# All edges gathered by indirect DMAs in tiles of 120 rows, and the gather on TensorE taken out

## The chip, the cores and the metric

The program runs on one core of a Trainium2 chip. The metric is the device time of one execution in microseconds (us). The kernel before has a median of 1892.74 us in 3 runs (1892.62 to 1893.34).

## What is computed

One layer of attention over the edges of a graph with 6250 nodes and 206250 edges (sorted by destination), 64 features in 4 heads of 16, then a residual and a layer norm:

```python
Qh = (x @ Wq.T + bq).reshape(n, H, D)
Kh = (x @ Wk.T + bk).reshape(n, H, D)
Vh = (x @ Wv.T + bv).reshape(n, H, D)
Ee = (edge_attr @ We.T + be).reshape(-1, H, D)
score = (Kh[src] * Qh[dst] * (1.0 / np.sqrt(D)) * Ee).sum(-1)
score = jnp.exp(jnp.clip(score, -5.0, 5.0))
msg = Vh[src] * score[..., None]
wV = jax.ops.segment_sum(msg, dst, num_segments=n)
# result: _layernorm(x + wV)
```

`src` is random, so K and V of the source nodes must be gathered row by row; `dst` is sorted, so the destinations of a run of edges lie in a narrow window.

## The kernel before

**Three stages.** The first block projects all nodes, writes K and V as one table of 512-byte rows to HBM (`kv_table`) and Q as a second table (`q_table`), and starts the first gathers. The middle block goes over the edges. The last block normalizes and stores.

**Tiles and groups.** A tile is 128 edges, one to a partition. T = 8 tiles make a group; the 1612 tiles make 202 groups, the last of 4 tiles. Group g uses slot g % 4 of four buffers (`kv`, `attr_sb`, `q_win`, `onehot`, `idx`).

**Two ways to gather.** GpSimd issues one indirect DMA for each tile: 128 rows of `kv_table` chosen by one column of `idx` (line 275, in `gather`). In slots 0, 1 and 3 the eighth tile of a group is not gathered by GpSimd: TensorE makes it by a product with a one-hot matrix over all 49 x 128 nodes (`pe_tile`, line 255). For such a tile VectorE makes the one-hot in four parts (line 803), TensorE multiplies it with the node features kept in three bf16 parts (49 products, line 675), turns the result (line 683) and projects it (line 689), and ScalarE copies between these steps (lines 765, 770, 776) and into `kv`. So GpSimd issues 1464 gathers, 7.25 for a group on average.

**What sets the order.** Each engine has its own hand-written order, and semaphores join them. GpSimd walks through the groups in order (line 612): for group g + 4 it waits for `slot_ready`, which VectorE raises when it has made the messages of group g and copied the new indices into `idx` (line 303). VectorE in group g waits for the slot's gathers (`kv_gathered`), for the tile of TensorE (`pe_kv_made`) and for the Q rows (`qe_made`), then does kq (824), adds the sums of the group before to `acc` (813), kqe (830), the reduction (835), the clip (839), waits for the exponential on ScalarE (772), makes the messages (844) and copies the indices. TensorE in group g makes the edge features and the turned one-hot of group g + 1 (625 to 633), fetches its Q rows (646) and sums the messages of group g (656). SyncE loads edge attributes and Q windows ahead, four slots deep.

**Around the middle block.** In the first block GpSimd issues 17 gathers of the first three groups (EARLY) and one reduction over partitions between them; it is the last engine to finish that block. `x_parts`, `columns`, `src_f` and `minus_first` serve the gather on TensorE alone and are made there on ScalarE, VectorE and GpSimd (lines 341, 418, 447 to 453, 524, 528).

Of the kernel before, what the change touches and what calls it, by code (L numbers as in the profile page):

```python
# [23 lines left out]
T = 8  # L49
PAIRS = T // 2  # L50
TILES = -(-E // P)
# [16 lines left out]
PE_TILES = ITERS * (SLOTS - 1) - 2  # L68
PARTS = tuple(slice(-(-NT * p // 4), -(-NT * (p + 1) // 4)) for p in range(4))
HALVES = (slice(0, (NT + 1) // 2), slice((NT + 1) // 2, NT))  # L70

PARTS_AT = (((0, 0), (0, 1), (0, 2)), ((0, 3), (1, 0), (1, 1)), ((1, 2), (1, 3), (2, 0)), ((2, 1), (2, 2), (2, 3)))
DONE_AT = (-1, None, 0, 1)
# [3 lines left out]
def gnn_kernel(nc, xT, x_own_rows, w_kvq, We_t, be_row, src_tab, dst_tab, dst_first, attr, out):  # L77
    ctx = ExitStack()
    with ctx:
# [6 lines left out]
        def sem(name):  # L86
# [9 lines left out]
        x_parts = sb("x_parts", [P, NT, 3, F], BF16)  # L96
# [10 lines left out]
        src_f = sb("src_f", [P, GPAD * T], F32)  # L107
        minus_first = sb("minus_first", [P, P], F32)
        columns = sb("columns", [P, NT, P], BF16)
# [6 lines left out]
        xg_t_sb = sb("xg_t_sb", [P, P], F32)  # L116
# [6 lines left out]
        x_own, x_rest = (kv_stage[:].rearrange("p t f -> p (t f)")[:, s * NT * F:(s + 1) * NT * F]  # L123
                         .rearrange("p (t f) -> p t f", f=F) for s in range(2))
# [15 lines left out]
        column_i = sb("column_i", [P, NT], I32, first)  # L140
        minus_first_i = sb("minus_first_i", [P, P], I32, first)
# [5 lines left out]
        xg_banks = [ps(f"xg_bank{i}", [P, 4, P], F32) for i in range(2)]  # L147
# [5 lines left out]
        src_ps = ps("src_ps", [P, 8, P], BF16)[:, 0, :]  # L153
        p_ps = sum_ps[:, 2, 0:T * H]
        xg_ps = [b[:].rearrange("p a b -> p (a b)")[:, 0:3 * F].rearrange("p (s f) -> p s f", s=3) for b in xg_banks]
        xg_t_ps = [b[0:F, 2, :] for b in xg_banks]
        xg_kv_ps = [b[:, 3, :] for b in xg_banks]

        kv_banks = [ee_ps[0], ee_ps[1], qe_ps, xg_banks[0]]
        q_banks = [oht_bank, sum_ps, xg_banks[1]]  # L160
# [16 lines left out]
        x_own_loaded = sem("x_own_loaded")  # L177
        x_part0 = sem("x_part0")
        x_rested = sem("x_rested")
        x_part1 = sem("x_part1")  # L180
        x_part2 = sem("x_part2")
# [5 lines left out]
        ident_zeroed = sem("ident_zeroed")  # L187
        ident_set = sem("ident_set")
        iota_set = sem("iota_set")
        column_set = sem("column_set")  # L190
# [48 lines left out]
        src_seen_made = sem("src_seen_made")  # L239
        src_turned = sem("src_turned")  # L240
        src_onehot_made = sem("src_onehot_made")
        x_gathered = sem("x_gathered")
        x_kept = sem("x_kept")
        x_turned = sem("x_turned")
        x_turned_kept = sem("x_turned_kept")
        kv_projected = sem("kv_projected")
        pe_kv_made = sem("pe_kv_made")
        window_moved = sem("window_moved")
        pass_sems = range(attr_loaded[0].num, window_moved.num + 1)
        assert len(pass_sems) == 3 * SLOTS + 26  # L250
# [4 lines left out]
        def pe_tile(g, slot):  # L255

            return slot != 2 and not (isinstance(g, int) and (g < 3 or g >= ITERS * SLOTS))

        def gathered_before(slot, turn):

            if isinstance(turn, int) and turn == 0:
                return 0
            if slot == 2:
                return turn * T

            return turn * (T - 1) + (1 if slot < 2 else 0)

        def pool_tiles(g, slot):

            return T - 1 if pe_tile(g, slot) else 2 * pairs_of(g)  # L270

        def gather(pool, g, slot, first=0, end=T):

# [6 lines left out]
        def is_tile(q):  # L280

            return not isinstance(q, int) or 0 <= q < PE_TILES

# [748 lines left out]
```

## Time and profile before

| | |
|---|---|
| median of 3 runs | 1892.74 us |
| span of the profiled execution | 2801.3 us |
| busy in it: PE, DVE, ACT, POOL | 1925.7, 1174.3, 851.7, 1400.8 us |
| gathers by GpSimd | 1464 |
| mean granted TensorE clock | 0.771 |

The profiled execution took 908.6 us longer than the median of the plain runs, far more than the runs differ among themselves. So a reader has to keep two things apart: the length of one instruction in it, and the waits between instructions, which need not be those of a plain run. PE stands for TensorE's products and PEld for its weight loads, DVE for VectorE, ACT for ScalarE, POOL for GpSimd, SP for SyncE. A gather counts as busy on POOL while GpSimd works on issuing it, 946 ns on average; its data moves later.

### The profile page before, as it was taken

The page shows a single profiled execution, that of the slowest core. Times are in us where ns is not written, and L with a number is a line of the kernel's source. Part 1 is how long each engine was busy: PE and PEld are TensorE (multiplying, and loading weights), DVE is VectorE, ACT ScalarE, POOL GpSimd, SP SyncE. Part 2 cuts the span into 40 slices and gives each one's busy share as a digit, 9 for nine tenths or more (in the row PEclk, how much of TensorE's full clock was granted, in tenths as well). Part 3 has the DMA queues.
Part 4 walks back from the last instruction along what each step waited for, and adds up shares of the span by engine and source line. Part 5 has one row for each costly group of instructions (what it writes and reads, how often), then busy time and mean ns, then how long its engine had stood idle before and what let it go on. Part 6 is the DMA issues. An engine that isn't in the chain of part 4 may idle for free. (4 is left out here: it accounts for less than half of the span.)

```text
span 2801.3 us, 49920 instructions
## 1 busy us (share of the span) xinstructions
PE 1925.7 (69%) x16647; PEld 1663.0 (59%) x16647; DVE 1174.3 (42%) x2092; ACT 851.7 (30%) x2863; POOL 1400.8 (50%) x1495
## 2 busy tenths in 40 slices
PE   4666677777767667776767676667676667766775
PEld 4555666666656556665656665656565656655665
DVE  4433444444434444444444444434344444434444
ACT  6222222332223223223322222223232223222233
POOL 5444554455554445555445555445545545555443
PEclk7777777777778777787877877778778777778776
DMA  6222222222222222222222222222222222222221
GB/s 194 63 56 57 59 58 58 57 61 57 58 54 59 56 58 60 58 59 59 59 57 58 59 57 58 57 56 60 57 58 58 59 57 60 59 58 59 56 61 45
DMA packets 113024, 171.42 MB, mean 61 GB/s; under 512 B 59952, under 2 KB 60592, under 8 KB 112880
## 3 DMA queue, kind: packets, MB, share of 16 engines
q0 software_dynamic: 46848, 96.04, 13.5%
q1 hardware_dynamic: 66160, 75.18, 9.8%
q8 instruction: 9, 0.15, 0.0%
q14 instruction: 7, 0.06, 0.0%
HBM read 163.85 MB, written 7.23 MB: 61 GB/s over the span
## 5 line engine op out<-in xcount | busy, mean ns | idle before, releaser
L275 POOL DMA_INDIRECT kv<-kv_table,idx x1464 | 1384.4, 946 | 1351.1 <-DVE idx L303 944.9
L675 PE MATMUL xg_bank<-x_parts,src_onehot 128*128 128x192 bf16 x7252 | 904.6, 286 | 102.7 <-issue 99.1
L675 PEld LDWEIGHTS xg_bank<-x_parts,src_onehot 128*128 128x128 bf16 x7252 | 739.8, 115 | 187.4 <-issue 129.2
L803 DVE TENSOR_TENSOR src_onehot<-src_ps,columns 128x1664 bf16<-128x1664 bf16 (+1 forms) x592 | 573.0, 968 | 537.0 <-remote 359.3
L646 PE MATMUL qe_ps<-q_win,onehot_t 128*128 128x128 bf16 x2418 | 250.2, 267 | 407.2 <-issue 389.9
L646 PEld LDWEIGHTS qe_ps<-q_win,onehot_t 128*128 128x128 bf16 x2418 | 194.3, 120 | 441.2 <-issue 439.5
L735 ACT COPY onehot_t<-oht_bank 128x512 bf16<-128x512 bf16 x202 | 118.0, 584 | 1099.3 <-remote 1052.4
L743 ACT ACTIVATE distance<-iota_w,dst_neg 128x64 f32<-128x64 f32 x1612 | 405.9, 337 | 15.4 <-PEq L306 15.4
L656 PE MATMUL sum_ps<-onehot,msg 128*64 128x64 f32 x3224 | 357.7, 290 | 49.3 <-issue 42.4
L656 PEld LDWEIGHTS sum_ps<-onehot,msg 128*64 128x64 f32 x3224 | 319.8, 200 | 111.1 <-issue 93.8
L844 DVE TENSOR_TENSOR msg<-kv,sum_ps 128x512 f32<-128x512 f32 x202 | 138.0, 683 | 563.2 <-ACT sum_ps L772 497.0
L633 PEld LDWEIGHTS ee_ps<-we_sb,attr_sb 128*128 128x128 f32 x1612 | 225.3, 201 | 16.9 <-issue 10.6
L633 PE MATMUL ee_ps<-we_sb,attr_sb 128*128 128x128 f32 x1612 | 228.5, 284 | 8.8 <-issue 8.1
L689 PE MATMUL xg_bank<-w_sb,xg_t_sb 128*128 128x128 f32 x296 | 106.7, 460 | 142.8 <-ACT xg_t_sb L770 113.8
L813 DVE TENSOR_TENSOR acc<-acc,sum_ps 64x64 f32 x202 | 43.2, 214 | 373.7 <-PE sum_ps L656 286.4
L824 DVE TENSOR_TENSOR kq<-kv,qe_ps 128x512 f32<-128x512 f32 x202 | 137.3, 680 | 125.3 <-ACT kv L776 82.6
L689 PEld LDWEIGHTS xg_bank<-w_sb,xg_t_sb 128*128 128x128 f32 x296 | 69.1, 289 | 180.4 <-ACT xg_t_sb L770 148.1
L770 ACT COPY xg_t_sb<-xg_bank 64x128 f32<-64x128 f32 x148 | 38.2, 258 | 330.7 <-remote 311.3
L830 DVE TENSOR_TENSOR kqe<-kq,ee_ps 128x512 f32<-128x512 f32 x202 | 136.3, 675 | 1.1 <-issue 0.3
L835 DVE TENSOR_REDUCE score<-kqe 128x32 f32<-128x512 f32 x202 | 135.5, 671 | 0.1
L748 ACT ACTIVATE onehot<-distance 128x512 f32<-128x512 f32 x202 | 127.0, 629 | 6.4
L765 ACT CAST xg_sb<-xg_bank 128x192 bf16<-128x192 f32 x148 | 45.0, 304 | 242.6 <-remote 228.8
(117 smaller groups left out, 760.9 us busy)
## 6 DMA issues: line engine op xcount, KB each, us to landing
attr_sb<-attr SPq DMA_DIRECT2D x201, 256.0 KB
kv<-kv_table,idx POOLq DMA_INDIRECT x1464
q_win<-q_table SPq DMA_DIRECT2D x404, 24.0 KB
kv_table<-kv_stage SPq DMA_DIRECT2D x7, 448.0 KB, 3.6
q_table<-q_stage SPq DMA_DIRECT2D x7, 336.0 KB
xT_sb<-xT SPq DMA_DIRECT2D x7, 224.0 KB, 4.8
kv_stage<-x_own_rows SPq DMA_DIRECT2D x1, 1568.0 KB
out<-y_sb SPq DMA_DIRECT2D x5, 256.0 KB, 2.0
```

Of the source, the lines that this page charges most:

```text
L275: pool.indirect_dma_start(out=kv[:, slot, t, :], out_offset=None, in_=kv_table, in_offset=bass.IndirectOffsetOnAxis(ap=idx[:, slot, t:t + ...
L633: mm = pe.matmul(ee[:, k * P:(k + 1) * P], attr_sb[:, slot, k * P:(k + 1) * P], we_sb[:, :], start=False, stop=(k == n - 1))
L646: mm = pe.matmul(bank(qe_ps, n * P)[:, k * P:(k + 1) * P], onehot_t[:, k, :], q_win[:, slot, :, s, :], start=(s == 0), stop=(s == 2))
L656: mm = pe.matmul(sum_ps[0:F, slot % 2, 0:W], msg[:, slot % 2, t, :], onehot[:, slot, t, :], start=(t == 0), stop=(t == n - 1))
L675: mm = pe.matmul(xg_ps[k % 2], src_onehot[:, c, :], x_parts[:, c, :, :], start=(c == 0), stop=(c == NT - 1))
L689: pe.matmul(xg_kv_ps[k % 2], xg_t_sb[:, :], w_sb[:, 0:2 * F], start=True, stop=True)\
L743: last = act.activation(distance[:, t, :], iota_w[:, :], ACT.Square, bias=dst_neg[:, ds(g, 1), t:t + 1].rearrange("p o t -> p (o t)"))
L803: dve.tensor_tensor(src_onehot[:, PARTS[part], :], src_ps.unsqueeze(1).to_broadcast([P, n, P]), columns[:, PARTS[part], :], ALU.is_equal). ...
L824: dve.tensor_tensor(kq[:, 0:n, :], kv[:, slot, 0:n, 0:F], qe_ps[:, 0:n, :], ALU.mult).then_inc(kq_made, 1)
L830: dve.tensor_tensor(kqe[:, 0:n, :], kq[:, 0:n, :], ee_ps[slot % 2][:, 0:n, :], ALU.mult).then_inc(kqe_made, 1)
L835: dve.tensor_reduce(score[:, 0:n * H], kqe[:, 0:n, :].rearrange("p t (h d) -> p (t h) d", d=D), AX_X, ALU.add).then_inc(score_summed, 1)
L844: dve.tensor_tensor(msg[:, slot % 2, 0:n, :].rearrange("p t (h d) -> p t h d", d=D), kv[:, slot, 0:n, F:2 * F].rearrange("p t (h d) -> p t ...
```

## The change

A tile has R = 120 edges, in partitions 0 to 119 of the 128. There are 1720 tiles in 215 groups, all of 8 tiles, and GpSimd gathers every one of them, 8 in each group. Everything that served the gather on TensorE is gone, in all three blocks. The host lays the tables out by 120 rows: rows 120 to 127 of a tile have an index and destination (copies of row 0) and edge attributes of zero, and a new memset clears rows 96 to 127 of `kv` once, before the gathers write rows 0 to 119. The other engines still compute on 128 rows of each tile.

```diff
+R = 120
-TILES = -(-E // P)
+TILES = -(-E // R)
+TILES += TILES % 2
...
-            for t in range(first, min(end, pool_tiles(g, slot))):
+            for t in range(first, min(end, 2 * pairs_of(g))):
                 pool.indirect_dma_start(
-                    out=kv[:, slot, t, :], out_offset=None, in_=kv_table,
-                    in_offset=bass.IndirectOffsetOnAxis(ap=idx[:, slot, t:t + 1], axis=0))\
+                    out=kv[0:R, slot, t, :], out_offset=None, in_=kv_table,
+                    in_offset=bass.IndirectOffsetOnAxis(ap=idx[0:R, slot, t:t + 1], axis=0))\
...
-                pool.iota(column_i[:, :], pattern=[[1, NT]], base=0, channel_multiplier=0).then_inc(column_set, 1)
+                pool.memset(kv[96:P, :, :, :], 0.0).then_inc(rows_zeroed, 1)
+                pool.wait_ge(rows_zeroed, 1)
...
-                        dve.wait_ge(kv_gathered[slot], 16 * (gathered_before(slot, i) + pool_tiles(g, slot)))
-                        if pe_tile(g, slot):
-                            dve.wait_ge(pe_kv_made, i * 3 + (-1, 0, None, 1)[slot])
+                        dve.wait_ge(kv_gathered[slot], 16 * (i * T + n))
...
-                        for part in parts[0:1]:
-                            make_src_onehot(*part)
...
-        padded = np.full(groups * T * P, fill, a.dtype)
-        padded[:E] = a
-        return np.ascontiguousarray(padded.reshape(groups * T, P).T)
+        real = np.full(groups * T * R, fill, a.dtype)
+        real[:E] = a
+        rows = np.full((groups * T, P), 0, a.dtype)
+        rows[:, :R] = real.reshape(-1, R)
+        rows[:, R:] = rows[:, :1]
```

On GpSimd, the loop of the middle block (four groups in a turn, one for each slot), before:

```order
L275 DMA kv<-kv_table,idx 128x128 x7
L602 REGISTER_ALU
L275 DMA kv<-kv_table,idx 128x128 x7
L602 REGISTER_ALU
L275 DMA kv<-kv_table,idx 128x128 x8
L602 REGISTER_ALU
L275 DMA kv<-kv_table,idx 128x128 x7
```

and now:

```order
L201 DMA kv<-kv_table,idx 120x128 x8
L470 REGISTER_ALU
L201 DMA kv<-kv_table,idx 120x128 x8
L470 REGISTER_ALU
L201 DMA kv<-kv_table,idx 120x128 x8
L470 REGISTER_ALU
L201 DMA kv<-kv_table,idx 120x128 x8
```

A turn has 32 gathers of 120 rows instead of 29 of 128, and nothing else on the engine moved.

On VectorE, one group of the loop, from kq to the copy of the indices, before:

```order
L824 TENSOR_TENSOR kq<-kv,qe_ps 128x512
...
L813 TENSOR_TENSOR acc<-acc,sum_ps 64x64
L830 TENSOR_TENSOR kqe<-kq,ee_ps 128x512
...
L803 TENSOR_TENSOR src_onehot<-src_ps,columns 128x1664
L835 TENSOR_REDUCE score<-kqe 128x32
L839 TENSOR_SCALAR score_c<-score 128x32
...
L803 TENSOR_TENSOR src_onehot<-src_ps,columns 128x1536
L844 TENSOR_TENSOR msg<-kv,sum_ps 128x512
...
L803 TENSOR_TENSOR src_onehot<-src_ps,columns 128x1536
...
L303 COPY idx<-src_sb 128x8
```

and now:

```order
L605 TENSOR_TENSOR kq<-kv,qe_ps 128x512
...
L597 TENSOR_TENSOR acc<-acc,sum_ps 64x64
L611 TENSOR_TENSOR kqe<-kq,ee_ps 128x512
L614 TENSOR_REDUCE score<-kqe 128x32
L618 TENSOR_SCALAR score_c<-score 128x32
L621 TENSOR_TENSOR msg<-kv,sum_ps 128x512
...
L207 COPY idx<-src_sb 128x8
```

The three one-hot steps of the group are gone, and the rest stands in the same order.

On TensorE, the same group of the loop, before:

```order
L625 MATMUL oht_bank<-ident_b,onehot 128x128 x4
L630 MATMUL ee_ps<-be_sb,ones 128x512
L633 MATMUL ee_ps<-we_sb,attr_sb 128x128 x4
L683 MATMUL xg_bank<-ident_b,xg_sb 64x128 x3
...
L675 MATMUL xg_bank<-x_parts,src_onehot 128x192 x12
...
L665 MATMUL src_ps<-ident_b,src_seen 128x128
L646 MATMUL qe_ps<-q_win,onehot_t 128x128 x12
L689 MATMUL xg_bank<-w_sb,xg_t_sb 128x128
...
L675 MATMUL xg_bank<-x_parts,src_onehot 128x192 x12
L656 MATMUL sum_ps<-onehot,msg 64x64 x8
```

and now:

```order
L493 MATMUL oht_bank<-ident_b,onehot 128x128 x4
L498 MATMUL ee_ps<-be_sb,ones 128x512
L501 MATMUL ee_ps<-we_sb,attr_sb 128x128 x4
L514 MATMUL qe_ps<-q_win,onehot_t 128x128 x12
L524 MATMUL sum_ps<-onehot,msg 64x64 x8
```

The 36 or 37 products of the one-hot gather in each group and the turns around them are gone.

## Rows read from the trace of the kernel before

**Rows 1.** The page: the span, and each engine's busy time.
```profile
span 2801.3 us, 49920 instructions
PE 1925.7 (69%) x16647; PEld 1663.0 (59%) x16647; DVE 1174.3 (42%) x2092; ACT 851.7 (30%) x2863; POOL 1400.8 (50%) x1495
```

**Rows 2.** Groups by line, POOL: busy and mean ns of one, idle before, releasers.
```profile
L275 POOL DMA_INDIRECT kv<-kv_table,idx x1464 | 1384.4, 946 | 1351.1 <-DVE idx L303 944.9 <-issue 399.6 <-DMA kv_table<-kv_stage 6.5
```

**Rows 3.** The page's costliest groups: work of the gather on TensorE, and VectorE's one-hot.
```profile
L675 PE MATMUL xg_bank<-x_parts,src_onehot 128*128 128x192 bf16 x7252 | 904.6, 286 | 102.7 <-issue 99.1
L803 DVE TENSOR_TENSOR src_onehot<-src_ps,columns 128x1664 bf16<-128x1664 bf16 (+1 forms) x592 | 573.0, 968 | 537.0 <-remote 359.3
```

**Rows 4.** Timeline, POOL: start and length in us, idle before. One run of 15 gathers.
```profile
163.16 0.94 POOL L275 DMA_INDIRECT kv<-kv_table,idx  x1 [3.57 <-DVE idx L303]
...
171.91 0.94 POOL L275 DMA_INDIRECT kv<-kv_table,idx  x1 [0.30 <-issue]
173.15 0.94 POOL L275 DMA_INDIRECT kv<-kv_table,idx  x1 [0.31 <-issue]
...
180.64 0.94 POOL L275 DMA_INDIRECT kv<-kv_table,idx  x1 [0.30 <-issue]
193.25 0.94 POOL L275 DMA_INDIRECT kv<-kv_table,idx  x1 [11.67 <-DVE idx L303]
```

**Rows 5.** Timeline, DVE, the same stretch: the group that runs from 162.29.
```profile
162.29 0.68 DVE L824 TENSOR_TENSOR kq<-kv,qe_ps 128x512 f32<-128x512 f32 x1
...
163.63 0.94 DVE L803 TENSOR_TENSOR src_onehot<-src_ps,columns 128x1536 bf16<-128x1536 bf16 x1
...
169.26 0.16 DVE L303 COPY idx<-src_sb 128x8 int32 x1
```

**Rows 6.** Timeline, all engines, from the first gathers to the middle block.
```profile
32.75 1.24 POOL L275 DMA_INDIRECT kv<-kv_table,idx  x1 [0.30 <-issue]
33.97 3.49 DVE L524 TENSOR_TENSOR kv_stage<-kv_stage,x_parts 128x1600 f32<-128x1600 f32 x2 [0.80 <-issue]
34.29 2.32 POOL L275 DMA_INDIRECT kv<-kv_table,idx  x1 [0.30 <-issue]
...
59.70 0.94 POOL L275 DMA_INDIRECT kv<-kv_table,idx  x1 [4.37 <-issue]
```

**Rows 7.** Timeline, all engines, the last groups and the end.
```profile
2759.15 0.94 POOL L275 DMA_INDIRECT kv<-kv_table,idx  x1 [0.30 <-issue]
...
2777.79 0.41 DVE L824 TENSOR_TENSOR kq<-kv,qe_ps 128x256 f32<-128x256 f32 x1
...
2791.61 7.66 SPq L984 DMA_DIRECT2D out<-y_sb  x7
...
2798.19 0.53 DVE L967 TENSOR_TENSOR y_sb<-c_sb,rstd 128x256 f32<-128x256 f32 x1
```

**Rows 8.** Timeline, PE: one group's work in the last stretch.
```profile
2761.85 0.61 PE L625 MATMUL oht_bank<-ident_b,onehot 128*128 128x128 bf16 x4
2762.25 0.63 PE L630 MATMUL ee_ps<-be_sb,ones 128*128 128x512 bf16 x1
2762.68 1.92 PE L633 MATMUL ee_ps<-we_sb,attr_sb 128*128 128x128 f32 x8
...
2764.98 1.46 PE L646 MATMUL qe_ps<-q_win,onehot_t 128*128 128x128 bf16 x12
...
2766.83 1.15 PE L656 MATMUL sum_ps<-onehot,msg 128*64 128x64 f32 x16
```

**Rows 9.** Waits by line: who waited for whom, us in total, times, longest.
```profile
ACT onehot_t L735 <- remote: 1052.4, 173, 14.3
```

**Rows 10.** Timeline, the first block before the gathers: GpSimd's memset, wait and first cast.
```profile
4.37 1.38 POOL L349 MEMSET q_win<- 128x1536 bf16 x1
...
13.73 0.24 POOL L360 CAST be_parts<-be_f 128x64 bf16<-128x64 f32 x1 [6.71 <-DMA be_f<-be_row]
```

**Rows 11.** The page's DMA queues: packets, MB, share of 16 engines.
```profile
q0 software_dynamic: 46848, 96.04, 13.5%
```

More of the change, by code:

```diff
@@ L66, with gnn_kernel @@
 assert CHUNKS * CH == NT and PASSES * W == NPAD and N < NPAD
[L68 to L73, printed above, removed]
 assert ITERS * SLOTS < G <= GPAD and TILES % 2 == 0 and SLOTS == 4
-def gnn_kernel(nc, xT, x_own_rows, w_kvq, We_t, be_row, src_tab, dst_tab, dst_first, attr, out):
+def gnn_kernel(nc, xT, w_kvq, We_t, be_row, src_tab, dst_tab, dst_first, attr, out):
     ctx = ExitStack()
@@ L176, in gnn_kernel @@
         be_loaded = sem("be_loaded")
[L177 to L181, printed above, removed]
         be_step = sem("be_step")
@@ L278, in gather @@
                     .then_inc(kv_gathered[slot], 16)
-        def is_tile(q):
-            return not isinstance(q, int) or 0 <= q < PE_TILES
-        def parts_at(i, j):
-            return [(i * 3 + k, k, part) for k, part in PARTS_AT[j] if is_tile(i * 3 + k)]
-        def done_at(i, j):
-            return i * 3 + DONE_AT[j] if DONE_AT[j] is not None and is_tile(i * 3 + DONE_AT[j]) else None
-        def turned_at(i, j):
-            return i * 3 + j if j >= 1 and is_tile(i * 3 + j) else None
@@ L692, in step @@
                     def step(g, i, j):
-                        parts, done, turned = parts_at(i, j), done_at(i, j), turned_at(i, j)
-                        ahead = not isinstance(g, int) or g + 1 < G
-                        if ahead:
+                        if not isinstance(g, int) or g + 1 < G:
                             edges_and_onehot(g + 1, (j + 1) % SLOTS, i + (j + 1) // SLOTS)
-                        if done is not None:
-                            turn_x(done, DONE_AT[j] % 3)
-                        early = 0 if j == 0 else 2
@@ L702, in step @@
-                        for part in parts[0:early][0:1]:
-                            gather_part(*part)
-                        if turned is not None and j < 3:
-                            turn_sources(turned)
-                        if ahead:
                             fetch_q(g + 1, (j + 1) % SLOTS, i + (j + 1) // SLOTS)
-                        if done is not None:
-                            project(done, DONE_AT[j] % 3)
-                        for part in parts[0:early][1:2]:
-                            gather_part(*part)
@@ L712, in step @@
                         sum_messages(g, j)
-                        for part in parts[early:]:
-                            gather_part(*part)
-                        if turned is not None and j == 3:
-                            turn_sources(turned)
                     edges_and_onehot(0, 0, 0)
                     fetch_q(0, 0, 0)
-                    turn_sources(0)
                     for g in range(SLOTS):
@@ L840, in step @@
                                           ALU.max, ALU.min).then_inc(score_clipped, 1)
-                        for part in parts[1:2]:
-                            make_src_onehot(*part)
                         dve.wait_ge(exp_made, g + 1)
@@ L848, in step @@
                                           ALU.mult).then_inc(msg_made, 1)
-                        for part in parts[2:3]:
-                            make_src_onehot(*part)
                         if not isinstance(g, int) or g + SLOTS < G:
```

154 lines of the change are left out of this document (19 added, 135 removed).

## The prediction

> **What bounds the kernel now.** The page comes first. Its span is 2801.3 us, 908.6 us over the plain median of 1892.74 us, and TensorE alone is busy for 1925.7 us in it [rows 1]. That is more than a whole plain run, so the profiled execution is not a picture of where a plain run waits. The view of waits says the same: ScalarE waits 1052.4 us for turned one-hots from TensorE [rows 9], and GpSimd stands idle before its gathers for 1351.1 us, 944.9 of it for indices from VectorE, which is late for the same reason [rows 2]. So I look for a path whose rows, without those waits, add up to a plain run.
>
> GpSimd's gathers are such a path. The timeline of one stretch where GpSimd did not wait shows 15 gathers that begin from 163.16 to 180.64, so a step is 17.48 / 14 = 1.2486 us: 0.944 of work and 0.304 of idle that no other engine ends [rows 4]. The stretch spans two groups, of 7 and 8 gathers or the reverse, and neither place where the border can lie (before 171.91 or before 173.15) costs anything extra. Five runs of 15 of this kind stand in the trace. The first gather of the middle block begins at 59.70 [rows 6], and 1464 - 17 = 1447 gathers follow from there: 1447 x 1.2486 = 1806.7, which gives 1866.4. After the last gather its data must land and one short group must be worked off. From that group's kq at 2777.79 to the end of the span are 23.5 us [rows 7]. Together 1889.9, against 1892.74: 2.8 us are left for the landing of the last gather. This agreement is my reason to say that a plain run is bound by GpSimd from the first gather to the last, and that the waits for indices are of the profiled execution alone.
>
> The next resource is VectorE's group: from kq at 162.29 to the end of the index copy at 169.42 are 7.1 us [rows 5], with the one-hots in it, against 7.25 x 1.2486 = 9.05 us of GpSimd. It is near, but under.
>
> **Part by part.** The plain time is 1464 x 1.2486 = 1828.0 us of gather steps and a rest of 64.7 us. I cost the change in these terms.
>
> *The gather on TensorE goes.* 7252 products of 904.6 us and 592 one-hot steps of VectorE of 573.0 us fall away [rows 3]. All of it lay beside GpSimd's steps, so I cost the removal at nothing. VectorE's group falls to about 7.1 - 3 x 0.968 = 4.2 us. TensorE keeps 0.61 + 0.63 + 1.92 + 1.46 + 1.15 = 5.8 us for a group in the slow stretch near the end [rows 8]. Both are far under 8 gather steps, so a colder clock on TensorE would not show.
>
> *More gathers.* 1720 instead of 1464, and 8 in each group, so GpSimd's group is 9.4 to 10.0 us and stays the bound.
>
> *A gather of 120 rows.* This is the term that decides, and the trace has only gathers of 128. The idle of 0.304 should stay. The 0.944 can be a cost of the instruction (then nothing is saved) or go with rows (then 0.944 x 120 / 128 = 0.885). The step is then between 1.189 and 1.249. If even the idle went with rows it would be 1.171. Neither end excludes a step in the cost: a gather puts 46848 / 1464 = 32 packets on the queue, two for each of 16 engines [rows 11], and 120 rows don't divide by 16, so the work may be laid out in another way, cheaper or dearer. I take 1.189, since a gather names its rows one by one, and most of a step is the busy time of just this. The gathers are then 1720 x 1.189 = 2045.1 us.
>
> The rows show 16 engines with a data packet of 8 rows each [rows 11]. The Trainium skill ("DMA: Bandwidth & Descriptors", section "Why a DMA increments its semaphore by 16 and not by 1") says that the number of engines is the largest one up to 16 that divides the slowest dimension; by it 120 rows go to 15 engines of 8 rows each, so that each engine's share is as before. Its section "Anatomy of one DMA" calls descriptor generation "small, variable"; by that the step would stay at 1.249 and the sum be the 2212 of the second case below.
>
> *The first block.* The two gathers at 32.75 and 34.29 take 1.24 and 2.32 us, beside VectorE's splitting of x (line 524) [rows 6], which goes: 0.30 + 1.38 = 1.7 us less. The new memset covers 4096 columns; at the rate of the one at 4.37 (1.38 us for 1536) it takes 3.7 us, and hides in the 6.7 us for which GpSimd then waits for the bias row [rows 10]. Without that cover it would be 3.7 us later. The other removed copies end before GpSimd's last early gather, and cost nothing now.
>
> *The end.* The last group has 8 tiles instead of 4. VectorE's four large steps take 0.68 instead of 0.41 each [rows 5, 7]: 1.1 us, and 8 more products some 0.4: 1.5 us more.
>
> Sum: 64.7 - 1.7 + 1.5 = 64.5, and 64.5 + 2045.1 = 2109.6 us, 11.5% over the time before. The time before is reached only if the step is (1892.7 - 64.5) / 1720 = 1.063 us or less: 0.186 us under 1.249, for 8 rows of 128.
>
> **The rivals.**
>
> *The row count doesn't matter.* Step 1.249: 64.5 + 2147.6 = 2212 us. For it: the lengths of 0.944 are so even that a large fixed part is likely. Against it: nothing in the rows.
>
> *A step down in the cost (faster).* If descriptors are made in batches, and 128 rows need one batch that 120 don't, the busy time falls by a whole batch. With four batches it would be 0.708 and the step 1.012: 64.5 + 1740.6 = 1805 us. With three: 0.629, 0.933 and 1669 us; with five the change breaks even. It decides at 1.063. For it: the borders of the work over 16 engines change at just this place, and when GpSimd's step falls, nothing else is near (VectorE 4.2, TensorE 5.8 us for a group). Against it: no row shows a batch.
>
> *The profiled step is too long (faster).* If a plain gather took well under 1.249, the kernel before would be bound by the chain of VectorE and TensorE instead, and taking their work away would free it. With a step of 1.05, 64.5 + 1806 = 1871 us or less. Against it stands that the sum over GpSimd meets the plain time to 3 us.
>
> *A dearer layout.* If 120 rows cost more than 128, the time is over 2212 us; with a tenth on the step, 2427 us.
>
> **How the numbers follow.** The step between 1.171 and 1.22 (2078 to 2163 us) has 0.35 and is the likeliest, with 2110; no gain from fewer rows (up to 2225) 0.17; a dearer gather 0.07; a cheaper one that is still slower than before (1.065 to 1.171) 0.06. That is 0.65 for slower. The step down has 0.28 and the too long profile 0.05, so 0.33 for faster; within 0.2%, which is about what a measurement of this kernel can tell from no change, 0.02. Since both signs hold a good part, the range goes from 1740 (a step of 0.974, within the case of batches) to 2225; it leaves out the dearer gather and the larger steps down. The likeliest case alone is 2070 to 2165.
>
> **What would show it.** In the profile after, the gathers' mean length against 946 ns is the deciding number: 885 for the forecast, 944 for a fixed cost, under 760 for faster. Gathers should follow each other at 0.30 us of idle across groups, so that POOL's idle before gathers falls from 1351 to some 540 us and waits for indices all but vanish. As TensorE has less than half the instructions, the profiled span should fall toward the plain time, although that rises: 2100 to 2250 us if the forecast holds. The packets of the queue tell how 120 rows are laid out (32 for a gather, or 31 with 15 engines). Wrong would be the forecast if the idle of 0.30 changes, if GpSimd waits for indices in spite of 4.2 us of work on VectorE, or if the gathers show two different lengths.

## The result, and the profile of the changed kernel

The changed kernel takes 2278.89 us (median of 4 runs, 2278.58 to 2279.27), the kernel before 1892.68 us (4 runs, 1892.25 to 1893.34): a ratio of 1.204, 95% interval [1.202, 1.206]. It is slower, as forecast, but by 386 us and not by 217, and 2279 lies above the range (1740 to 2225).

One thing has to be said for the rest to be understood: the plain runs of these kernels are of one of two kinds, the same for all that were made together, here called short (the kernel before takes 1892 to 1893 us) and long (it takes 2792 to 2814 us); the comparison on record is of the short kind, all experiments but E9 to E12 are of the long kind, and so, by its span of 2801.3 us, is the trace of before.

The page of the changed kernel (span and busy times; two groups by line; the queue of the gathers):

```profile
span 2276.8 us, 32362 instructions
PE 1225.7 (54%) x8952; PEld 1105.0 (49%) x9060; DVE 736.6 (32%) x1586; ACT 752.5 (33%) x2411; POOL 1709.5 (75%) x1749
...
q0 software_dynamic: 55040, 105.84, 17.2%
...
L201 POOL DMA_INDIRECT kv<-kv_table,idx x1720 | 1690.0, 983 | 534.4 <-issue 522.1
...
L605 DVE TENSOR_TENSOR kq<-kv,qe_ps 128x512 f32<-128x512 f32 x215 | 147.9, 688 | 1360.8 <-DMA kv<-kv_table,idx 1340.4
```

The line of the gathers (L201) answers to [rows 2]. There are 1720 of them, and one has GpSimd busy for 983 ns, where it was 946. Of the idle time before them, 522.1 us of 534.4 are the step's own ("issue"); of the 944.9 us of waiting for indices 6.1 are left. The last line shows that VectorE now waits for gathered rows in nearly every group. GpSimd's row of gathers is the bound.

The timeline of GpSimd in the middle (start and length in us, idle before), which answers to [rows 4]:

```profile
1000.87 0.98 POOL L201 DMA_INDIRECT kv<-kv_table,idx  x1 [0.30 <-issue]
1002.16 0.98 POOL L201 DMA_INDIRECT kv<-kv_table,idx  x1 [0.31 <-issue]
1003.44 0.98 POOL L201 DMA_INDIRECT kv<-kv_table,idx  x1 [0.30 <-issue]
...
1011.17 0.98 POOL L201 DMA_INDIRECT kv<-kv_table,idx  x1 [0.30 <-issue]
```

From 1000.87 to 1011.17 are 8 steps (those between are alike): 1.2875 us each. Over the 34 steps from 1000.87 to 1044.61 it is 1.2865 (over all 1702 steps of the middle block, from 59.14 to 2248.49, 1.2863), and no border between two groups costs anything extra. 1720 x 1.2865 = 2212.8 us, which leaves 66.1 us of 2278.9 for all the rest; the forecast had 64.5 there. So the sum has one term wrong, the step.

The end of the kernel, which answers to [rows 7]:

```profile
2248.49 0.98 POOL L201 DMA_INDIRECT kv<-kv_table,idx  x1 [0.31 <-issue]
2251.92 0.69 DVE L605 TENSOR_TENSOR kq<-kv,qe_ps 128x512 f32<-128x512 f32 x1 [7.32 <-DMA kv<-kv_table,idx]
```

The last gather begins 28.3 us before the end of the span and the last group's kq 24.9 us before it, against 23.5 in [rows 7].

### The profile page after: what moved, and what is told of

Same layout as the page of the kernel before. It is cut to its first block and busy times, and to the rows that moved or that the text cites. A ratio compares the mean times of both kernels' runs of the same rounds, so it can differ in the third digit from the quotient of the medians.

```text
span 2276.8 us, 32362 instructions
## 1 busy us (share of the span) xinstructions
PE 1225.7 (54%) x8952; PEld 1105.0 (49%) x9060; DVE 736.6 (32%) x1586; ACT 752.5 (33%) x2411; POOL 1709.5 (75%) x1749
## 5 line engine op out<-in xcount | busy, mean ns | idle before, releaser
L201 POOL DMA_INDIRECT kv<-kv_table,idx x1720 | 1690.0, 983 | 534.4 <-issue 522.1
L524 PE MATMUL sum_ps<-onehot,msg 128*64 128x64 f32 x3440 | 420.7, 316 | 350.0 <-DVE msg L621 350.0
L524 PEld LDWEIGHTS sum_ps<-onehot,msg 128*64 128x64 f32 x3440 | 380.6, 223 | 402.5 <-DVE msg L621 402.5
L573 ACT ACTIVATE sum_ps<-score_c 128x32 f32<-128x32 f32 x215 | 43.2, 201 | 1313.7 <-DVE score_c L618 1313.7
L501 PEld LDWEIGHTS ee_ps<-we_sb,attr_sb 128*128 128x128 f32 x1720 | 385.9, 308 | 19.1
L501 PE MATMUL ee_ps<-we_sb,attr_sb 128*128 128x128 f32 x1720 | 367.0, 386 | 24.0 <-issue 23.0
L493 PE MATMUL oht_bank<-ident_b,onehot 128*128 128x128 bf16 x860 | 130.0, 306 | 32.2 <-ACT onehot L564 32.2
L493 PEld LDWEIGHTS oht_bank<-ident_b,onehot 128*128 128x128 bf16 x860 | 73.6, 130 | 57.3 <-ACT onehot L564 32.7
L498 PE MATMUL ee_ps<-be_sb,ones 128*128 128x512 bf16 x107 | 67.6, 632 | 0.0
L618 DVE TENSOR_SCALAR score_c<-score 128x32 f32<-128x32 f32 x215 | 42.4, 197 | 7.5
```

The lines of the kernel that those rows point to most:

```text
L201: pool.indirect_dma_start(out=kv[0:R, slot, t, :], out_offset=None, in_=kv_table, in_offset=bass.IndirectOffsetOnAxis(ap=idx[0:R, slot, t: ...
L493: mm = pe.transpose(oht_ps[:, k, :], onehot_b[:, slot, k, :], ident_b[:, :])
L501: mm = pe.matmul(ee[:, k * P:(k + 1) * P], attr_sb[:, slot, k * P:(k + 1) * P], we_sb[:, :], start=False, stop=(k == n - 1))
L524: mm = pe.matmul(sum_ps[0:F, slot % 2, 0:W], msg[:, slot % 2, t, :], onehot[:, slot, t, :], start=(t == 0), stop=(t == n - 1))
```

## The experiments

Three questions were put. What does a gather of another number of rows cost? Is the row of gathers the bound, in this direction and in the other? And how do the 386 us split? All kernels with fewer or other rows are the kernel after with these lines changed:

```diff
-                    out=kv[0:R, slot, t, :], out_offset=None, in_=kv_table,
-                    in_offset=bass.IndirectOffsetOnAxis(ap=idx[0:R, slot, t:t + 1], axis=0))\
+                    out=kv[0:GR, slot, t, :], out_offset=None, in_=kv_table,
+                    in_offset=bass.IndirectOffsetOnAxis(ap=idx[0:GR, slot, t:t + 1], axis=0))\
```

Where GR is under 120, the rows above GR are zeros and their edges are left out (in E8 the memset of `kv` begins at row 64 for this). Where it is over 120, the rows above 120 fetch the source node of the tile's first edge again; their edge attributes are zero, but not the bias, so they add to that node's sums.

**E1. Tiles of 128, all by GpSimd.** The kernel after with one number changed. 1612 gathers; the whole reference is computed.

```diff
-R = 120
+R = 128
```

> The changed kernel with tiles of 128 edges: 1612 gathers of 128 rows, all by GpSimd, no gather on TensorE, the whole reference computed. Theory (the price of a gather hangs on its row count and on nothing else in the change): the gathers take 944 ns as in the kernel before, the step is 1.2486 us, and with the rest of 64.6 us the time is 1612 x 1.2486 + 64.6 = 2077 us. Rival (the price rose because of what was taken off the other engines, or because GpSimd now works without a pause): 983 ns as in the changed kernel, a step of 1.2865 and 2138 us. If TensorE's gather had been a cost in the kernel before, the time would lie under 2077.

Measured: 2749.3 us, and the kernel before beside it 2803.6 us (7 runs, 2793 to 2812): 0.981 [0.977, 0.984]. The runs were of the long kind, where neither time of the expectation applies. The group of the gathers:

```profile
L201 POOL DMA_INDIRECT kv<-kv_table,idx x1612 | 1527.2, 947 | 1163.3 <-DVE idx L207 691.9 <-issue 465.4 <-DMA kv_table<-kv_stage 6.0
```

The gather is back at 947 ns in the new kernel, so the 983 belong to the 120 rows and not to anything else of the change.

**E2. 128 rows for each tile of 120.** GR = 128. The expectation says that the extra rows add nothing; in fact they add to the sums. The instructions are the same either way.

> The changed kernel with its 1720 tiles of 120 edges, but each gather takes 128 rows (the last 8 are copies of the tile's first index, which add nothing to the result). Theory (row count alone): 944 ns, step 1.2486, 1720 x 1.2486 + 66.1 = 2214 us, 65 us faster than with 120 rows, although 7% more bytes move. Rival (the price comes with the change's other parts): 983 ns and 2279 us, as the changed kernel.

Measured: 2931.1 us, 1.046 [1.042, 1.050], long kind; the gather 947 ns. The price moved as expected, the time can't be judged here.

**E3 and E4. 112 and 105 rows.** GR = 112 (16 x 7) and GR = 105 (15 x 7).

> The changed kernel, 1720 gathers of 112 rows (16 engines x 7): rows 112 to 119 of each tile are not gathered, so part of the edges is left out. Theory A (a row costs 944 / 128 = 7.4 ns, and 120 is dear only because it doesn't divide over 16 engines): 826 ns, step 1.130, 2010 us. Theory B (a fixed price for each instruction): 944 ns, 2214 us. Anything between gives the price of a row: (944 - busy) / 16.

> The changed kernel, 1720 gathers of 105 rows (15 x 7): rows 105 to 119 of each tile are not gathered. Theory (a layout over 15 engines costs about 39 ns more than one over 16 with the same rows for each engine, as 120 against 128 does, 983 against 944): busy is that of the 112-row gather plus 39 ns. Rival (the 39 ns are a thing of 120 rows or of 8 rows an engine alone): busy at or under that of the 112-row gather. The queue should show 15 data packets of 3584 bytes and a small one for each gather.

Measured: 2932.7 and 2939.5 us (one run each, long kind). The groups of the gathers, first of E3, then of E4:

```profile
L202 POOL DMA_INDIRECT kv<-kv_table,idx x1720 | 1611.8, 937 | 1258.5 <-DVE idx L208 747.1 <-issue 504.6 <-DMA kv_table<-kv_stage 6.8
```

```profile
L202 POOL DMA_INDIRECT kv<-kv_table,idx x1720 | 1673.1, 973 | 1203.6 <-DVE idx L208 701.3 <-issue 495.8 <-DMA kv_table<-kv_stage 6.5
```

Sixteen rows fewer, still divisible by 16, save 9 ns. Seven rows fewer than that, and not divisible, cost 36 ns more. So E3 came out near its theory B, a fixed price, and E4 as its theory said (976 expected). The price has a small part that goes with rows and a part that depends on how the rows divide.

**E5 and E6. The kernel after and E1 once more.** Nothing is changed in them. They ask whether the long kind meets every kernel, or came from something in E1 and E2.

> The changed kernel itself, beside the kernel before on one chip. In the four runs before this one, the kernel before took 2804 us instead of 1893, the kernels with all gathers on GpSimd 2749 to 2939 us, and in their traces single register instructions of SyncE last 0.69 us while GpSimd gathers in a row. Theory S1 (a state of the chip or of the job that meets every kernel): if this job meets it too, before is near 2800 and this 2930 to 2940, like the gathers of 105 rows; if not, before is near 1893 and this near 2279, with gathers of 983 ns in either case. Theory S2 (120 rows escape it): this near 2279 with before near 2800.

> Tiles of 128 edges, 1612 gathers of 128 rows, all by GpSimd, once more, to have it beside the changed kernel on one chip. Where the kernel before takes 1893 us: theory (only the gathers' count and price matter) 1612 x 1.251 + 64.6 = 2081 us, 9.9% over before and 197 us under the changed kernel, of which 139 us are the 108 further gathers and 58 us the higher price. Rival (the work taken off TensorE is worth something in the plain run too): under 2060. Where before takes 2800: near 2749 again.

Measured: 2920.9 us for the kernel after, 1.042 [1.039, 1.046], where the record has 2278.9; 2748.4 for E1's kernel, 0.980 [0.977, 0.983]; the kernel before 2801.8 beside them. So the long kind isn't a thing of E1's kernel or of other row counts: the kernel after and the kernel before have it too. The gathers are 983 and 945 ns there. The 983 are those of the short kind, so the price of a gather can be read in either kind.

**E7 and E8. 104 and 64 rows.** GR = 104 (13 x 8) and GR = 64 (16 x 4).

> 1720 gathers of 104 rows of each tile of 120 (rows 104 to 119 are left out). 104 = 13 x 8. So far 128 rows take 947 ns, 112 take 937, 120 take 983 and 105 take 973: 0.6 ns for a row, and 36 to 41 ns more where 16 does not divide the rows. Theory K1 (one fixed surcharge for a layout on fewer than 16 engines): 932 + 40 = 972 ns, and one small packet of 32 bytes for each gather. Theory K2 (a surcharge for each engine left out): 932 + 3 x 40 = 1050 ns and three small packets.

> 1720 gathers of 64 rows of each tile of 120 (rows 64 to 119 are left out). 64 = 16 x 4. Theory (0.6 ns for a row, the rest a fixed price of the instruction): 947 - 64 x 0.62 = 907 ns, a step of 1.211 and 2149 us where the kernel before takes 1893, so a gather of half the rows saves 3% of its time. Rival (the price of rows grows only beyond some count, or the 112-row value was chance): anything from 700 to 947.

Measured: 985 and 904 ns (2908.4 and 2944.8 us, one run each, long kind). E8's group of gathers:

```profile
L202 POOL DMA_INDIRECT kv<-kv_table,idx x1720 | 1554.0, 904 | 1323.7 <-DVE idx L208 738.1 <-issue 579.1 <-DMA kv_table<-kv_stage 6.5
```

64 rows came out as the line through 128 and 112 said. At 104 rows three engines are left out and the surcharge is 55 ns, neither the 42 of one engine (K1) nor three times that (K2).

**E9 and E10. What holds the kernel of E1.** E1's kernel with the Q rows loaded for the first four groups only (later groups use stale Q rows), and with 14 matmuls of a group left out (one slice of q instead of three, two tiles summed instead of eight). E9:

```diff
+                        if not isinstance(g, int) or g >= SLOTS:
+                            return
                         rows = q_table[ds(base, W), :].rearrange("n (s f) -> n s f", s=3)
...
-                        pe.wait_ge(q_loaded[slot], 32 * (turn + 1))
+                        pe.wait_ge(q_loaded[slot], 32)
```

E10:

```diff
-                            for s in range(3):
-                                mm = pe.matmul(bank(qe_ps, n * P)[:, k * P:(k + 1) * P],
-                                               onehot_t[:, k, :], q_win[:, slot, :, s, :],
-                                               start=(s == 0), stop=(s == 2))
+                            mm = pe.matmul(bank(qe_ps, n * P)[:, k * P:(k + 1) * P],
+                                           onehot_t[:, k, :], q_win[:, slot, :, 0, :],
+                                           start=True, stop=True)
...
-                        for t in range(n):
+                        for t in range(2):
```

> All edges gathered by GpSimd in tiles of 128 (1612 gathers), and the two loads of a group's q rows are left out after the first four groups (their 25,700 or so DMA packets of 117,600; the q used for the later groups is then a stale window). Question: what holds the all-GpSimd kernel at 2749 us where its 1612 gathers alone would take 1612 x 1.251 = 2017 us. Theory P (the number of DMA packets: all eight runs on this chip state came to 42.5 to 43.0 packets per us): (117,600 - 25,700) / 42.8 = 2147 us. Theory N (the engines' instruction streams, which crawl while gathers are issued back to back, whatever the number of packets): as before within 2%, 2700 to 2760 us. Gather price 946 ns by both. If the kernel before comes out at 1893 us in this job instead of 2803 us, both give the gather bound, 1612 x 1.251 + 64.6 = 2081 us, and the run shows that bound instead.

> All edges gathered by GpSimd in tiles of 128 (1612 gathers), with 14 matmuls of a group left out: one of three slices of q per pair of tiles (4 instead of 12) and two of eight tiles summed (so most messages are left out of the sums); 2814 fewer TensorE instructions, the packets the same 117,600. Theory P (packets): 2749 us within 1%. Theory N (instruction streams that crawl): TensorE's share of the chain from a gather burst's end to the next one gets shorter; by the 0.69 us per instruction seen in a burst 14 matmuls are up to 9.7 us of a group's 13.6, so 2749 falls to 2500 or below. If the kernel before is at 1893 us in this job: 2081 us by both.

Measured: 2076.7 and 2076.2 us (one run each), with the kernel before at 1892.6 us (7 runs, 1892.5 to 1893.2): the short kind, so their question on the long kind stays unanswered, and they show the bound instead. The gathers of E9:

```profile
L201 POOL DMA_INDIRECT kv<-kv_table,idx x1612 | 1523.7, 945 | 500.6 <-issue 494.0
```

117,600 packets or 85,900, 8507 weight loads or 4479, the time is the same to 0.5 us, and it is 1612 x 1.2486 + 64.5 = 2077.2. Neither of the two pieces of work that were left out weighs anything beside the gathers in the short kind.

**E11. The kernel before with 50 gathers fewer.** In slot 2 GpSimd gathers seven tiles too. The eighth is left out there (zeros, so its edges add nothing).

```diff
             if slot == 2:
-                return turn * T
+                return turn * (T - 1)
...
+            if slot == 2:
+                return T - 1 if not isinstance(g, int) or g < ITERS * SLOTS else 2 * pairs_of(g)
             return T - 1 if pe_tile(g, slot) else 2 * pairs_of(g)
```

> The kernel before, where GpSimd gathers seven tiles of eight in the third of every four groups too (the eighth is left out there: its k and v are zeros, so its edges add nothing): 50 gathers fewer, nothing else changed. Theory: the kernel before is bound by its row of gathers, so 50 x 1.249 = 62 us fall away whole: 1893 - 62 = 1830 us, ratio 0.967. Rival: another engine's loop ends next and keeps part, 1850 to 1893. In a job where the kernel before takes 2803 us the gathers are not the bound: by packets (50 x 32 of 112,900) 2803 - 40 = 2763, ratio 0.986.

Measured: 1830.4 us (4 runs, 1830.3 to 1830.6), ratio 0.967 [0.966, 0.969]: the expected number. Its page is the only one here that shows the kernel before's design in the short kind:

```profile
span 1828.7 us, 49624 instructions
PE 1475.5 (81%) x16448; PEld 1364.1 (75%) x16647; DVE 1174.4 (64%) x2092; ACT 866.2 (47%) x2863; POOL 1354.2 (74%) x1446
...
L277 POOL DMA_INDIRECT kv<-kv_table,idx x1414 | 1337.7, 946 | 440.6 <-issue 433.1 <-DMA kv_table<-kv_stage 6.0 <-DVE idx L305 1.5
```

With all the work of the gather on TensorE in place, GpSimd waits 1.5 us for indices in the whole run, against 944.9 us in [rows 2]. So this work does hide behind the gathers in the short kind, and the 50 gathers are worth 62.2 / 50 = 1.244 us each.

**E12. 126 rows.** GR = 126.

> The kernel after, but 126 rows of each tile of 120 edges gathered instead of 120 (the six extra rows repeat an edge of the tile and add to its sums). Question: the price of one gather when 16 does not divide its rows. Law A (0.65 ns per row on 862 ns, plus 42 ns at 120 and 105 rows, plus 55 at 104): 126 splits as 14 engines x 9 rows, so 944 + 42 to 55 = 986 to 999 ns, with packets of 14 x 4608 B and fillers for the two engines left over. Law B (the surcharge follows the engines left out, 42 for one, so 84 for two): 1028 ns. Law C (the price follows bytes only; 120 is an oddity): 944 ns.

Measured: 2303.2 us (one run, short kind). The queue and the group of the gathers:

```profile
q0 software_dynamic: 82560, 111.19, 19.0%
...
L202 POOL DMA_INDIRECT kv<-kv_table,idx x1720 | 1713.7, 996 | 535.2 <-issue 523.5 <-DMA kv_table<-kv_stage 7.8 <-DVE idx L208 4.0
```

996 ns is law A's number, 32 below law B's. The trace lists for each gather 14 packets of 4096 bytes, 14 of 512, 2 of 32 and 18 of 4, 48 in all: 14 shares of 9 rows, each in two pieces. So the surcharge doesn't follow the number of packets (48 here, 32 at 104 rows with 55 ns). The run also shows that a dearer gather reaches the end nearly one for one: against the kernel after, 13 ns x 1720 = 22.4 us, and the time rose by 24.3 us.

**E13 to E18. The two directions, and the split again.** E13 and E16 are one kernel, which computes the whole reference: TensorE makes the eighth tile of every group, slot 2 included (198 tiles instead of 148), all four parts of a tile in one group, and GpSimd has 1414 gathers.

```diff
-PE_TILES = ITERS * (SLOTS - 1) - 2
+PE_TILES = ITERS * SLOTS - 2
...
-            return slot != 2 and not (isinstance(g, int) and (g < 3 or g >= ITERS * SLOTS))
+            return not (isinstance(g, int) and (g < 2 or g >= ITERS * SLOTS))
...
-            return [(i * 3 + k, k, part) for k, part in PARTS_AT[j] if is_tile(i * 3 + k)]
+            q = i * SLOTS + j
+            return [(q, j, part) for part in range(4)] if is_tile(q) else []
```

E14 and E17 are E1's kernel, E15 and E18 are E2's.

> The kernel before, extended the other way: TensorE gathers one tile of every group of eight (198 tiles instead of 148), so GpSimd has 1414 gathers of 128 rows. The whole reference is computed. By the bound that the run with 1414 gathers showed (1830.4 us with that tile left out): 1414 x 1.249 + 64.6 = 1831 us, ratio 0.967, if TensorE and VectorE keep up. Rival: TensorE (1475 us busy there, about 2.2 us more for each of 50 tiles, 1585) or VectorE (1174 + about 75) or the waits between them end later than the seven gathers of a group (8.74 us): 1835 to 1900. If the kernel before takes 2803 us in this job, the comparison shows little: 0.97 to 1.02.

> All edges gathered by GpSimd in tiles of 128: 1612 gathers, the whole reference computed. Splits the +386 us of the change. By the sum: 1612 x 1.251 + 64.6 = 2081 us (two kernels like it, with work left out, came to 2076 and 2077), ratio 1.10: so 148 gathers more (what TensorE had done) are 185 us of the 386, and the tiles of 120 with their dearer gather the rest, 200. Rival: something else than the gathers is in the 386, so this lies 10 us or more away from 2076 to 2081. If the kernel before takes 2803 us in this job: 2749 as twice before.

> The kernel after, but each of the 1720 gathers fetches 128 rows for its tile of 120 edges (the eight extra rows add to the sums of a node). Takes the surcharge of the 120-row form away and leaves the count: 1720 x (0.946 + 0.304) + 66 = 2216 us, 63 us less than the kernel after although it gathers more rows. Rival: the 983 ns come from the shorter tile in another way (its place in the queue, the waits), so it stays at 2279 or above.

> The kernel of e13 again (TensorE gathers a tile of every group, 1414 gathers left, the whole reference computed), for a job where the kernel before takes 1893 us as in the comparison on record: 1414 x 1.249 + 64.6 = 1831 us, ratio 0.967, if TensorE and VectorE keep up; if one of them is the bound, 1835 to 1900. In a job where the kernel before takes 2803 us: 2970 again.

> The kernel of e1 and e14 again (1612 gathers of 128 rows, the whole reference computed): 1612 x 1.251 + 64.6 = 2081 us, ratio 1.10, where the kernel before takes 1893 us; else 2748.

> The kernel of e2 and e15 again (1720 gathers of 128 rows for tiles of 120 edges, the eight extra rows add to the sums): 1720 x (0.946 + 0.304) + 66 = 2216 us where the kernel before takes 1893 us, 63 us less than the kernel after; else 2930.

All six were of the long kind (the kernel before 2802.7 and 2802.4 us). E13 and E16: 2969.5 and 2971.7 us (2945 to 3000 among nine runs), 1.057 [1.048, 1.067] and 1.061 [1.058, 1.065]; the expectation of E13 had 0.97 to 1.02 for the long kind, so that was a miss. E14 and E17: 2746.9 and 2746.7 us, 0.980 [0.977, 0.983] and 0.981 [0.978, 0.984]. E15 and E18: 2929.3 and 2929.8 us, 1.045 [1.041, 1.048] and 1.046 [1.042, 1.051]. They repeat E1 and E2 closely, and what they were to show in the short kind stays unmeasured: whether TensorE and VectorE keep up with a tile in every group is open, and so is E2's kernel's own 2216.

## Why the prediction was right or wrong

**The price of a gather of 120 rows: wrong.** This is the step that failed. The prediction scaled the busy time of 0.944 us with the rows and took 0.885; the trace has 0.983. All prices that were measured:

| rows | engines x rows | busy, mean ns | over the line |
|---|---|---|---|
| 128 | 16 x 8 | 946 (before), 945 to 948 | 0 |
| 112 | 16 x 7 | 937 (E3) | +2 |
| 64 | 16 x 4 | 904 (E8) | 0 |
| 126 | 14 x 9 | 996 (E12) | +51 |
| 120 | 15 x 8 | 983 (after, E5) | +42 |
| 105 | 15 x 7 | 973 (E4) | +42 |
| 104 | 13 x 8 | 985 (E7) | +55 |

The line goes through 128 and 64 rows: (946 - 904) / 64 = 0.66 ns for a row, on 862 ns that don't go with rows (what lies below 64 rows was not tried). Eight rows fewer are worth 5 ns, not 59. On top comes a surcharge of 42 to 55 ns at the four row counts that 16 doesn't divide. So two things were wrong at once: the part that goes with rows is a tenth of what was assumed, and the layout costs. Of the forecast's argument "a gather names its rows one by one, and most of a step is the busy time of just this" only the 0.66 ns for a row are left. The evenness of the 0.944 us, which the prediction put on the side of a large fixed part and then passed over, was the better guide.

The split itself shows in the packets of the queue. For each gather of the kernel after the trace lists 15 packets of 4096 bytes, one of 32 and 16 of 4: fifteen shares of eight rows of 512 bytes, and a small one in the sixteenth's place, so 32 packets as in [rows 11]. At 104 rows it is 13 of 4096 and three of 32, at 105 rows 15 of 3584 and one of 28; at 112 rows there are 16 of 3584 and no small one. (The prediction had 31 packets in mind for 15 engines.) The rule that the prediction cited from the Trainium skill ("DMA: Bandwidth & Descriptors", section "Why a DMA increments its semaphore by 16 and not by 1"), by which the number of engines is the largest up to 16 that divides the rows, agrees with all seven row counts. The same section of the Trainium skill says that for such a DMA all 16 engines post their count, whatever its shape. The 16 packets of 4 bytes that stand beside 15 shares fit that; why there are 18 at 126 rows is open. The prediction drew from the rule that each engine's share is as before, and stopped there. It did not ask what GpSimd does for the engine that gets nothing. The surcharge grows with the engines that get no share, though less than in step: 42 ns for one, 51 for two, 55 for three. It isn't set by what is left over when the rows are divided by 16 alone: that is 8 for both 120 and 104 rows. What takes the 42 ns inside the gather, the small packets or another path of the instruction, was not separated.

**The rival "the row count doesn't matter": nearer than the forecast.** It gave 2212 us. The prediction named for it the words "small, variable", by which the Trainium skill ("DMA: Bandwidth & Descriptors", section "Anatomy of one DMA") describes descriptor generation. The 0.66 ns for a row agrees with them; how much of the 862 ns is descriptor generation no run here shows.

**The rival "a dearer layout": this is what happened.** It had a chance of 0.07 and no size but the remark of "a tenth on the step". The size is 3% on the step: 1.2865 / 1.2486 = 1.030, so 0.0379 x 1720 = 65.2 us over the flat case. The range ended at 2225, between the flat case and this one. The prediction said itself that neither end excludes a step in the cost and that 120 rows could be dearer; a range that took this in would have had to reach 67 us above 2212. The sign came out right by the count: the break-even was a step of 1.063 us, and the cheapest gather measured, 64 rows, has 0.904 + 0.304 = 1.208.

**The steps down and the too long profile: not seen.** The price has no step of hundreds of ns between 64 and 128 rows, and the step of 1.2486 read in the long kind holds in the short one. In E9 the gathers of the middle block begin from 58.43 to 2048.27, 1594 steps of 1.2483 us:

```profile
58.43 0.94 POOL L201 DMA_INDIRECT kv<-kv_table,idx  x1 [4.36 <-issue]
...
2048.27 0.94 POOL L201 DMA_INDIRECT kv<-kv_table,idx  x1 [0.30 <-issue]
```

E11, the kernel before and E9 lie at 1414, 1464 and 1612 gathers with 1830.4, 1892.6 and 2076.7 us, which is 1.244 us for a gather between each two.

**What bounds the kernel: right, with a wrong reason for the profile.** The sum over GpSimd's gathers met the time before to 3 us, and E11 confirms it by a change of its own. But the prediction laid the 908.6 us of the trace, and its waits for indices, to the profiled execution. The profiled execution of the kernel after has a span of 2276.8 us, the same as its plain runs (2276.9 to 2277.5). In the long kind the plain runs of the kernel before have spans of 2790 to 2813 us at a granted clock of 0.768 to 0.778, and the trace of before has 2801.3 us and 0.771. So it matches an execution of the long kind, and nothing is left for the profiling to explain. Why it is of another kind than the plain runs that stand beside it is not shown. The forecast "the profiled span should fall toward the plain time" came true by the kind of the execution, not by fewer instructions on TensorE as it had said.

**The removal at nothing: right.** In the short kind E11's page (1.5 us of waiting for indices) and E9 and E10 (the end doesn't move with TensorE's or SyncE's work) show it. The mean granted clock of TensorE fell from between 0.91 and 0.92 in the kernel before (its runs beside E9 to E12) to 0.632 in the kernel after, so it spent a large part of the time at the lower of its two levels (1.2 of 2.4 GHz). It made no difference, as said: E9 with 0.637 and E10 with 0.551 take the same time.

**The idle of 0.304 us stays: right.** 1.2865 - 0.983 = 0.3035, and 0.30 to 0.31 at every row count. POOL's idle before gathers was forecast at some 540 us and is 534.4.

**The first block and the end: right.** The memset was put at 3.7 us, hidden under the wait for the bias row. It takes 3.51, and that wait is 4.20 us now where it was 6.71 [rows 10]; the cast behind it begins 0.42 us later:

```profile
3.16 3.51 POOL L248 MEMSET kv<- 32x4096 f32 x1
...
14.15 0.24 POOL L261 CAST be_parts<-be_f 128x64 bf16<-128x64 f32 x1 [4.20 <-DMA be_f<-be_row]
```

The last group was put at 1.5 us more; from kq to the end it is 24.9 - 23.5 = 1.4. The 1.7 us for lengthened early gathers came only in part: in the new trace two gathers at 30.60 and 31.95 take 1.04 and 1.26 us, 0.3 more than the usual 0.98 together. All that is not a gather step came to 66.1 us against 64.5.

**Where the 386 us are.** From the kernel before to 1612 gathers of 128 rows (what TensorE had done): 2076.7 - 1892.7 = 184.0 us, measured with E9. The 108 gathers that tiles of 120 add: 108 x 1.2486 = 134.8 us. The dearer gather: 0.0379 x 1720 = 65.2 us. Together 384.0 of 386.2. The first part is measured on E9, where the loads of the Q rows are left out; E10, which keeps them and leaves out other work, comes to the same time. E1's kernel as a whole was never measured in the short kind. The other two parts are worked out from counts and prices that were each measured.

## What to carry to other kernels

When one engine issues DMAs back to back and is the bound, the number of DMAs is what costs: here 1.25 us each, of which eight rows of 128 are 5 ns. Making such a gather smaller saves next to nothing (half the rows, 42 of 946 ns), and the row counts here that don't split over 16 engines cost 4 to 6% more on the instruction, so by the price of the instruction 128 rows for a tile of 120 are cheaper than 120 (946 against 983 ns). Work that takes DMAs off such an engine and hides behind the rest is worth its trouble: the gather on TensorE saved 184 us in the short kind (in the long kind it cost 55). Before a profile's extra time is put down to the profiling, look for plain runs that are as slow.

## What the runs showed of the hardware that was not expected

**In the long kind the other engines nearly stand still late in a row of gathers.** A group's start of gathers in E1 (timeline, all engines; SPq is SyncE's queue; "remote" is a releaser that the profile doesn't name):

```profile
1011.59 0.27 PE L501 MATMUL ee_ps<-we_sb,attr_sb 128*128 128x128 f32 x1 [1.06 <-issue]
...
1013.10 0.69 DVE L605 TENSOR_TENSOR kq<-kv,qe_ps 128x512 f32<-128x512 f32 x1 [5.92 <-remote]
...
1021.50 0.70 SPq L451 DMA_DIRECT2D q_win<-q_table  x1
1021.86 0.94 POOL L201 DMA_INDIRECT kv<-kv_table,idx  x1 [0.30 <-issue]
1025.87 0.59 ACT L551 COPY onehot_t<-oht_bank 128x512 bf16<-128x512 bf16 x1 [17.15 <-remote]
1025.91 0.21 DVE L597 TENSOR_TENSOR acc<-acc,sum_ps 64x64 f32 x1 [12.13 <-remote]
1026.05 0.67 DVE L611 TENSOR_TENSOR kqe<-kq,ee_ps 128x512 f32<-128x512 f32 x1
...
1029.73 0.94 POOL L201 DMA_INDIRECT kv<-kv_table,idx  x1 [6.93 <-DVE idx L207]
```

The same steps of a group in the kernel after, short kind:

```profile
1006.14 0.69 DVE L605 TENSOR_TENSOR kq<-kv,qe_ps 128x512 f32<-128x512 f32 x1 [6.33 <-DMA kv<-kv_table,idx]
...
1007.05 0.21 DVE L597 TENSOR_TENSOR acc<-acc,sum_ps 64x64 f32 x1 [0.23 <-issue]
1007.19 0.67 DVE L611 TENSOR_TENSOR kqe<-kq,ee_ps 128x512 f32<-128x512 f32 x1
...
1009.92 0.17 DVE L207 COPY idx<-src_sb 128x8 int32 x1 [0.16 <-DVE msg L621]
```

From kq to the next step of VectorE are 12.1 us of idle in the first and 0.23 in the second, with the same instructions of the same length. In E1 the stop begins some 8 us into a row of 16 gathers (they start at 1003.10) and ends 4 us after the last one begins (1021.86 to 1025.87); in between VectorE does one step and SyncE issues three DMAs. Then VectorE catches up and GpSimd waits 6.93 us for its indices. SyncE's instructions that only count, compare or branch (the trace holds them, the views leave them out) take 0.69 to 0.70 us each in the stop, where a count takes 0.04 us outside of it.

The kernel after itself can be compared in both kinds. Its gathers in the long kind (E5):

```profile
L201 POOL DMA_INDIRECT kv<-kv_table,idx x1720 | 1690.5, 983 | 1163.2 <-DVE idx L207 662.8 <-issue 493.9 <-DMA kv_table<-kv_stage 6.5
```

The idle time before gathers is 1163.2 us against 534.4, and these 628.8 us are nearly all of the 636.8 us between the spans (2913.6 and 2276.8). The gathers themselves are as long as before; what grows is GpSimd's waiting for indices from engines that were held up.

This makes the long kind a different problem. There 1612 gathers take 2748 us and 1720 take 2921, E8's cheaper gather (904 ns) buys nothing (2945 us), and E13's kernel, with 50 more tiles on TensorE and its one-hot steps in another order, takes 167 to 169 us more than the kernel before. Taking the gather off TensorE with tiles of 128 comes out 2% under the kernel before (0.980 [0.977, 0.983], and 0.980 or 0.981 in all four comparisons), where in the short kind it costs 184 us. What the stop consists of is open. The total of DMA packets over the span is nearly constant among the kernels in which GpSimd gathers all (first E1, 42.8 packets per us, then E8, 42.5, with 65 and 46 GB/s, so it isn't bytes; the gathers per us are as constant, 0.587 and 0.584, so these kernels don't tell packets from gathers):

```profile
DMA packets 117612, 179.46 MB, mean 65 GB/s; under 512 B 62304, under 2 KB 62944, under 8 KB 117600
```

```profile
DMA packets 125022, 134.50 MB, mean 46 GB/s; under 512 B 66320, under 2 KB 66832, under 8 KB 125008
```

But E13, with 111,426 packets and 55,680 instructions in a span of 2951.9 us, has 37.7, so packets alone are not the law. E9 and E10 were made to tell packets from instructions and were of the short kind; no run of the long kind with fewer packets for the same gathers was made. What puts an execution into one kind or the other is open too. The five sets of runs in which the experiments were made were on five chips, and the one in the short kind (E9 to E12) was alone on its chip, so chip and chance aren't told apart.
